# Rows h and -h added and subtracted ahead of the transform along h; that transform in 64x64 tiles, and one signal per unit in the second mixing

## What is computed

```python
residual = x
h = layer_norm(x, n1_g, n1_b)
xf = rfft2(h, axes=(1, 2), norm='ortho')          # 65 frequencies along w, 128 along h
# eight blocks of 16 channels, complex:
o1r = relu(xr @ w1[0] - xi @ w1[1] + b1[0]);  o1i = relu(xi @ w1[0] + xr @ w1[1] + b1[1])
o2r = softshrink(o1r @ w2[0] - o1i @ w2[1] + b2[0]);  o2i = softshrink(o1i @ w2[0] + o1r @ w2[1] + b2[1])
y = irfft2(o2r + 1j * o2i) + h
h = y + residual
residual = h
h = layer_norm(h, n2_g, n2_b)
return gelu(h @ mw1 + mb1) @ mw2 + mb2 + residual
```

## Time and profile before

| what | value |
|---|---|
| median of 3 runs | 1629.3 us (1629.04 to 1630.48) |
| the profiled execution | 1629.48 us |
| its span in the profile | 1627.7 us |
| TensorE matmul busy | 1556.1 us, 96% of the span |
| VectorE busy | 990.3 us, 61% |
| ScalarE busy | 889.3 us, 55% |
| POOL busy | 620.4 us, 38% |
| DMA, mean | 85 GB/s |

### The profile page before, as it was taken

How to read it: one execution, slowest core, us unless ns; L and a number is a source line. 1 busy time by engine, 2 the same in 40 slices (tenths; PEclk the granted TensorE clock), 3 DMA queues, 4 the chain that set the end, 5 groups by cost and what they waited for, 6 DMA issues and landing times.

```text
span 1627.7 us, 43919 instructions
## 1 busy us (share of the span) xinstructions
PE 1556.1 (96%) x16132; PEld 1379.1 (85%) x16132; DVE 990.3 (61%) x2433; ACT 889.3 (55%) x1638; POOL 620.4 (38%) x782
## 2 busy tenths in 40 slices
PE   0999999999999899999999989999999989999999
PEld 0987888888998788888898888888889879888888
DVE  7967556656537665665655766565663675555553
ACT  5544366666534356666643436666662443666665
POOL 5800046776800017677660003667673000111111
PEclk9999999999999999999999999999999999999999
DMA  8410713333300062333420052333331006011111
GB/s 225 172 45 3 241 49 107 104 99 119 98 15 3 9 240 86 108 101 99 124 79 2 3 203 66 104 110 97 104 111 46 3 3 207 27 39 32 32 39 46
DMA packets 168583, 138.30 MB, mean 85 GB/s; under 512 B 10882, under 2 KB 132484, under 8 KB 168452
## 3 DMA queue, kind: packets, MB, share of 16 engines
q1 hardware_dynamic: 167268, 136.24, 26.6%
q10 hardware_dynamic: 1184, 0.20, 0.1%
HBM read 69.30 MB, written 67.11 MB: 84 GB/s over the span
## 4 chain that ended last, share of the span: by engine, by line
PE 93%; DVE 3%; ACT 1%; SPq 1%; DMA 1%; issue 1%; POOL 0%; ACTq 0%; DVEq 0%
PE ps L797 27%; PE ps L591 8%; PE ps L611 8%; PE ps L581 7%; PE ps L763 7%; PE ps L765 7%; PE ps L724 7%; PE ps L764 7%; PE ps L757 3%; PE ps L649 3%; PE ps L743 3%; PE ps L749 3%; SPq L431 1%; DMA first<-in_x_dram 1%; PE ps L779 1%
## 5 line engine op out<-in xcount | busy, mean ns | idle before, releaser
L797 PEld LDWEIGHTS ps<-mw,gel 128*128 128x128 f32 x4000 | 520.6, 191 | 42.3
L797 PE MATMUL ps<-mw,gel 128*128 128x128 f32 x4000 | 523.7, 274 | 0.0
L907 ACT ACTIVATE gel<-ps,mb1f 128x512 f32<-128x512 f32 x500 | 343.7, 687 | 250.6 <-PE ps L765 219.7
L1473 POOL TENSOR_TENSOR arena<-arena,mb2rep 128x512 f32<-128x512 f32 x125 | 160.2, 1282 | 634.5 <-ACT hn L893 634.5
L763 PE MATMUL ps<-hth,mw1h 128*128 128x512 f32 x512 | 259.7, 507 | 4.5 <-DVE vsb L1119 1.7
L1462 POOL TENSOR_SCALAR arena<-xnext,rstd,shift 128x128 f32<-128x128 f32 x360 | 159.4, 462 | 207.6 <-DVE shift L1356 207.6
L893 ACT ACTIVATE hn<-arena,shift,rstd 128x128 f32 (+1 forms) x512 | 221.6, 483 | 16.8 <-DVE shift L1356 16.8
L765 PE MATMUL ps<-hth,mw1l 128*128 128x512 f32 x512 | 202.1, 395 | 0.0
L764 PE MATMUL ps<-htl,mw1h 128*128 128x512 f32 x512 | 200.8, 392 | 0.0
L1203 DVE TENSOR_TENSOR arena<-ps,arena 128x512 f32 (+1 forms) x60 | 41.5, 691 | 252.0 <-PE ps L749 233.4
L871 ACT COPY gsb<-ps 128x512 f32<-128x512 f32 x128 | 69.1, 589 | 159.1 <-PE ps L611 153.0
(11 more groups left out here) (111 smaller groups left out, 2125.6 us busy)
## 6 DMA issues: line engine op xcount, KB each, us to landing
arena<-aside SPq DMA_DIRECT2D x128, 256.0 KB, 4.8
aside<-gz SPq DMA_DIRECT2D x96, 256.0 KB, 3.0
between<-xout SPq DMA_DIRECT2D x62, 256.0 KB, 2.3
out_dram<-xout SPq DMA_DIRECT2D x62, 256.0 KB, 2.3
xnext<-between SPq DMA_DIRECT2D x60, 256.0 KB, 3.0
aside<-first SPq DMA_DIRECT2D x32, 256.0 KB, 2.3
xnext<-in_x_dram SPq DMA_DIRECT2D x30, 256.0 KB, 3.1
first<-in_x_dram SPq DMA_DIRECT2D x1, 960.0 KB, 7.4
```

The costliest lines, as they stand in the source:

```text
L797: mm = pe.matmul(ps[:, r % 2, P * i:P * i + P], gel[:, r % 2, m, P * i:P * i + P], mw2[:, s // IMAGES, m, :], start=(m == 0 and i == 0), s ...
L907: act.activation(gel[:, r % 2, m, :], ps[:, 2 + m % 2], ACT.Gelu, bias=mb1f[:, s // IMAGES, m:m + 1]).then_inc(gelu_out, 1)
L1473: pool.tensor_tensor(t, t, b, ALU.add).then_inc(mb2_done, 1)
```

## The change

- In steps 1 to 3 the slots 64 to 127 of an image are written in mirrored order (`zplace`, and the row order in `z_rows`, `scale` and VectorE's last tiles), so that slot 64 + i holds the row that is minus the row of slot i. The inverse constants are mirrored too, and the second half of the inverse transform along w reads its rows forward.
- The transform along w of steps 1 to 3 (`mirrored`) makes, for each four channels of both halves of the spectrum's rows, one bank from the slots 0 to 63 and one from the slots 64 to 127. Each matmul has 64 stationary columns, and two of them (g = 0 and 1) fill the two halves of the bank's partitions.
- ScalarE copies the first bank of the two to `hn` as it is (`upper_copy`), and VectorE writes the sum and the difference of that copy and the second bank into the spectrum (`fold_out`, two operations for each pair of banks). TensorE waits for VectorE's signal alone.
- The transform along h of steps 1 to 3 works on 64 partitions of sums and 64 of differences with the constants `FOLDS` (65 and 95 columns), in 64x64 tiles, for both units of a pair at once. It waits once, for both copies. The first two units are still done one by one.
- `mix2` uses banks 4 and 5 for q = 0 and 6 and 7 for q = 1, signals each unit, and waits for the first `shrink` operation of the same q in the pair before. `edges` stands ahead of mix2(4), whose second unit waits for VectorE's `edges_out`.
- The order of the frequencies along h is even ones first, then odd ones. The held products use banks 2 and 3, and `idft_h` waits for their GELUs.
- Step 0 keeps the transform along w and the 128x128 transform along h as they are.

The core of the diff:

```diff
@@ -73,8 +73,10 @@
 MASKS = 4 * BLOCKS
-CONSTS = 7 * P + MASKS
 EVEN = KWS + 1
+FOLD_E, FOLD_O = EVEN, P - EVEN + KWS // 2
+MASK_AT = 7 * P + FOLD_E + FOLD_O
+CONSTS = MASK_AT + MASKS
...
@@ -90,7 +92,7 @@
 HELD = TILES - 1
-HELD_BANK = (6, 7, 0, 2)
+HELD_BANK = (2, 3, 0, 2)
...
@@ -111,10 +113,18 @@
     fw[:, 0, 1] = cos[:, KWS]
-    fh = np.concatenate([np.cos(turn * np.outer(h, k)), np.sin(turn * np.outer(h, k[1:-1]))], 1) * scale
-    k_of = np.concatenate([k, -k[1:-1]])
+    ks = np.concatenate([[0, KWS], np.arange(2, KWS, 2), np.arange(1, KWS, 2)])
+    fh = np.concatenate([np.cos(turn * np.outer(h, ks)), np.sin(turn * np.outer(h, ks[2:]))], 1) * scale
+    k_of = np.concatenate([ks, -ks[2:]])
+
+    fold_e, fold_o = fh[:HALF, :EVEN].copy(), fh[:HALF, P - FOLD_O:].copy()
+    fold_e[-1] = scale * (ks % 2 == 0)
+    fold_o[:, :KWS // 2] = 0
+    fold_o[-1] = -scale * (np.arange(FOLD_O) < KWS // 2)
+    folds = np.tile(np.concatenate([fold_e, fold_o], 1), (2, 1))
     ih = np.concatenate([np.cos(turn * np.outer(k_of, h[:HALF + 1])),
                          np.sin(turn * np.outer(k_of, -h[HALF + 1:]))], 1) * scale
+    ih[:, HALF:] = ih[:, :HALF - 1:-1].copy()
 
...
@@ -182,6 +192,7 @@
         paired = [a.rearrange("p (t h e) -> p t h e", h=H, e=2) for a in flat]
...
@@ -207,7 +222,8 @@
         FW, FH, IH, DE, DO, IDENT, REVERSE = (cst[:, i * P:(i + 1) * P] for i in range(7))
-        mask = cst[:, 7 * P:].rearrange("p (s b) -> p s b", s=4)
+        FOLDS = tuple(cst[:, 7 * P + a:7 * P + b] for a, b in ((0, FOLD_E), (FOLD_E, FOLD_E + FOLD_O)))
+        mask = cst[:, MASK_AT:].rearrange("p (s b) -> p s b", s=4)
...
@@ -378,6 +394,11 @@
             return rows_of(s)[:, :, bass.ds(h0, ROWS), :].rearrange("p t h e -> p h t e")
+
+        def zplace(j, r):
+
+
+            return (2 * j + r // 2 + TILES // 2) * ROWS if r % 2 else tile_of(j, r) * ROWS
...
@@ -556,10 +577,8 @@
                     pe.wait_ge(a_act, cg + 1)
-                elif cg % 2:
-                    pe.wait_ge(a_dve, CGROUPS // 2 * (s - 1) + cg // 2 + 1)
-                else:
-                    pe.wait_ge(a_act, CGROUPS + CGROUPS // 2 * (s - 1) + cg // 2 + 1)
+                else:
+                    pe.wait_ge(a_dve, CGROUPS * (s - 1) + cg + 1)
...
@@ -573,8 +592,9 @@
                 for cg in range(CGROUPS):
-                    if s and cg == 3:
-                        pe.wait_ge(lo_out, TILES * s)
+                    if s:
+                        mirrored(s, cg // 2, cg % 2)
...
@@ -582,7 +602,45 @@
                                        start=True, stop=True)
                     mm.then_inc(s1_mm, 1)
 
-            def dft_h(s, n):
+            def mirrored(s, d, sign):
+
+                if d == 1 and sign:
+                    pe.wait_ge(lo_out, TILES * s)
+                if d >= 2 and not sign:
+                    evicted(s, 2 * d - 3)
+                q, slots = d // 8, slice(HALF, H) if sign else slice(0, HALF)
+                for i in range(GROUP):
+                    for g in range(2):
+                        t = KWS // 2 * q + KWS // 4 * g + GROUP // 2 * (d % 8) + i // 2
+                        mm = pe.matmul(ps[HALF * g:HALF * g + HALF, 2 + 2 * (d % 2) + sign, P * i:P * i + P],
+                                       rows_of(s)[:, t, slots, i % 2], FW, start=(i == 0), stop=True,
+                                       skip_group_check=True)
+                mm.then_inc(s1_mm, 1)
+
+            def dft_h(s, n, units=(0,)):
+                if s:
+                    g = spectrum_of(n + units[-1])
+                    if g >= 2:
+                        pe.wait_ge(g_out, 2 * BATCHES * s + g - 1)
+                    for i in range(GROUP):
+                        for o in range(2):
+                            for u in units:
+                                q = (n + u) % 2
+                                for x in range(2):
+                                    own_rows = slice(HALF * x, HALF * x + HALF)
+                                    cols = slice(HALF * (x ^ q), HALF * (x ^ q) + HALF)
+                                    dst = slice(P * i, P * i + EVEN) if o == 0 else slice(P * (i + 1) - FOLD_O, P * (i + 1))
+                                    mm = pe.matmul(ps[cols, q, dst],
+                                                   folded_of(s)[own_rows, GROUP * (g // 2) + i, o, q].rearrange(
+                                                       "p r c -> p (r c)"),
+                                                   FOLDS[o][own_rows], start=(i == 0 and o == 0), stop=True,
+                                                   skip_group_check=True)
...
@@ -635,20 +693,22 @@
                 kws = 1 if p == 1 else GROUP
-                if s == 0 and p == 1:
-                    pe.wait_ge(r_dve, R_DVE)
-                if p >= 2:
-                    pe.wait_ge(v_out, UNITS * s + 2 * p - 2)
                 for q in range(2):
+                    if p:
+                        pe.wait_ge(v_out, UNITS * s + 2 * p + q - 1)
+                    elif s == 0 and q:
+                        pe.wait_ge(r_dve, R_DVE)
+                    if p == EDGE_PAIR and q:
+                        pe.wait_ge(y_done, (UNITS + 1) * s + 2 * EDGE_PAIR + 1)
                     pe.wait_ge(o_out, UNITS * s + 2 * p + q + 1)
                     for i in range(kws):
-                        at_ = GROUP * HALF * q + HALF * i
+                        at_ = HALF * i
                         for c in range(2):
                             for g in range(2):
                                 own_rows, k = slice(HALF * g, HALF * (g + 1)), slice(HALF * c, HALF * (c + 1))
-                                mm = pe.matmul(ps[k, 4 + 2 * (p % 2) + g, at_:at_ + HALF], osb[own_rows, q, i, k],
+                                mm = pe.matmul(ps[k, 4 + 2 * q + g, at_:at_ + HALF], osb[own_rows, q, i, k],
                                                w2s[own_rows, q].rearrange("p r c -> p (r c)"), start=True, stop=True)
-                mm.then_inc(m2_mm, 2)
+                    mm.then_inc(m2_mm, 1)
 
...
@@ -660,25 +720,21 @@
                 mix1(s, 0)
-                for q in range(2):
-                    dft_h(s, 4 + q)
+                dft_h(s, 4, (0, 1))
                 for p in range(PAIRED):
                     if p + 1 < PAIRED:
                         mix1(s, p + 1)
-                    if p == EDGE_PAIR + 1:
-                        pe.wait_ge(y_done, (UNITS + 1) * s + 2 * EDGE_PAIR + 2)
-                    mix2(s, p)
                     if p == EDGE_PAIR:
                         edges(s)
+                    mix2(s, p)
                     if p + 3 < PAIRED:
-                        for q in range(2):
-                            dft_h(s, 2 * p + 6 + q)
+                        dft_h(s, 2 * p + 6, (0, 1))
                 if s:
                     fc1_held(s, 0)
                     fc1_held(s, 1)
                 else:
                     pe.wait_ge(v_out, UNITS * s + UNITS - 2)
-                    keep_warm(8, 6)
...
@@ -719,6 +775,8 @@
                         turned(s, cg - 4)
+                    elif s and cg >= 2:
+                        pe.wait_ge(gelu_out, CHUNKS * (TILES * s - 1) + cg - 1)
...
@@ -864,6 +922,11 @@
 
+            def upper_copy(s, q, j, r):
+
+                act.wait_ge(s1_mm, CGROUPS * s + CGROUPS // 2 * q + 4 * j + 2 * r + 1)
+                act.copy(hn[:, r].rearrange("p a b -> p (a b)"), ps[:, 2 + 2 * r]).then_inc(a_act, 1)
+
...
@@ -929,11 +992,17 @@
                     act.wait_ge(mb2_done, TILES * s)
-                for q in range(2):
-                    for g in range(2):
-                        with act.Fori(0, CGROUPS // 16) as j:
-                            for r in ((0, 2) if s else range(4)):
-                                a_out(s, q, g, j, r)
+                if s == 0:
+                    for q in range(2):
+                        for g in range(2):
+                            with act.Fori(0, CGROUPS // 16) as j:
+                                for r in range(4):
+                                    a_out(s, q, g, j, r)
+                else:
+                    for q in range(2):
+                        with act.Fori(0, CGROUPS // 8) as j:
+                            for r in range(2):
...
@@ -1087,9 +1156,15 @@
 
-            def a_out(s, q, g, j, r):
-                dve.wait_ge(s1_mm, CGROUPS * s + CGROUPS // 2 * q + CGROUPS // 4 * g + 4 * j + r + 1)
-                evict_a(dve.tensor_copy, s, q, g, 4 * j + r, r).then_inc(a_dve, 1)
+            def fold_out(s, q, j, r):
+
+                dve.wait_ge(a_act, CGROUPS + CGROUPS // 2 * (s - 1) + CGROUPS // 4 * q + 2 * j + r + 1)
+                dve.wait_ge(s1_mm, CGROUPS * s + CGROUPS // 2 * q + 4 * j + 2 * r + 2)
+                upper = hn[:, r].rearrange("p a b -> p (a b)").rearrange("p (i k r) -> p k r i", i=GROUP, r=2)
+                lower_ = ps[:, 3 + 2 * r].rearrange("p (i k r) -> p k r i", i=GROUP, r=2)
```

(43 more changed lines are left out.)

45 lines of the change are left out of this document (23 added, 22 removed).

## The result

The changed kernel takes 1639.8 us (median of 4 runs, 1636.66 to 1640.32) against 1629.2 us on the same chip. The ratio is 1.0059, 95% interval 1.0042 to 1.0077: about 10 us slower, where 1613.5 us and "faster" were forecast.

What follows compares the result with a forecast made beforehand. TensorE, busy 96% of the span, was taken as the bound, with ScalarE's chain next in the filter's pairs. 12.2 + 0.7 - 0.2 + 1.9 + 1.4 = 16.0 us off 1629.5 gave 1613.5 us; range 1602 to 1626.

Steps and rivals of the forecast that it cites:

- The step that failed: Transform along w, steps 1 to 3: VectorE's sum and difference fit under TensorE's time; the stage nets 1.4 us won.
- second rival: Transform along w: VectorE's sum and difference, 1.2 us each, become the bound; 33 us more, 1646 us; chance 0.05.
- the way to mix1(0): From the start of the transform along w to the first mixing, steps 1 to 3: 1.3 us lost in all.
- Mixing to `idft_h`: Filter from mix1(0) to the start of `idft_h`, steps 1 to 3: 17.4 us won in all.
- Undisturbed pairs: Filter's middle pairs, steps 1 to 3: from 4.79 to 4.41 us, bound by ScalarE's copies and relus; 12.2 us won.
- the prediction's own signs of being wrong: TensorE waiting for VectorE in most bank pairs, a pair at 4.0 or 4.8 us, or first mixing waiting for copies.
- First rival: Transform along w: 128-row column tiles run one after another, 90 us more in three steps, 1705 us; chance 0.05.
- Third rival: Folded transform along h: bound by issue, 1.6 us, pair stays 4.78 us, 12.2 us gone, 1625.5 us; chance 0.06.
- Fourth rival: Filter's pairs: ScalarE's chain does not bind, a pair falls to TensorE's 3.98 us, kernel 1599 us; chance 0.06.
- Edges: Edges in the filter: 0.1 us won in each of steps 1 to 3, 0.5 lost in step 0; net loss 0.2.
- Tail: End of the filter, all four steps: a signal for each unit starts the inverse 0.47 us earlier; 1.9 us won.
- Step 2: Transform along w in step 2: weight scaling between the halves stalls TensorE for some 0.6 us.

Runs made afterwards that it cites:

- Experiment 1: The changed kernel with ScalarE's copy writing `hn` in the order in which VectorE reads it: 1619.84 us, ratio 0.9942 to the kernel before.
- experiment 10: experiment 5 run once more, on the chip of experiment 9: 1609.43 us, ratio 0.9874.
- experiment 5: Experiment 1 without the 95-column half of the folded transform along h, from the third pair on in steps 1 to 3: 1609.58 us, ratio 0.9876.
- experiment 6: experiment 5 with ScalarE's relus working on half the columns in all steps: 1588.35 us in a single execution.
- experiment 3: The kernel before with only the second mixing's part (banks by q, signal per unit, edges ahead of mix2(4), held products in banks 2 and 3): 1630.59 us.
- experiment 8: Experiment 1 run once more, on the chip of experiment 7: 1619.48 us, ratio 0.9934.
- experiment 7: Experiment 1 with the edges back behind mix2(4), written to the unused upper half of bank 6: 1618.37 us, ratio 0.9933.
- experiment 9: experiment 5 with the left-out matmuls issued again, each with one column instead of 95: 1616.49 us, ratio 0.9927.

## Why the prediction was wrong

- **The step that failed: "128x512 with two operands takes 690 ns, also where it writes strided, so 1.5 us with addressing, under the 1.85 us that TensorE needs for two banks."** The row writes short runs and reads SBUF in plain order; the new operation also reads SBUF with neighbours 512 bytes apart, and no row had that. It took 1070 ns, a bank pair 2.14 us. This is the second rival, "VectorE's sum and difference become the bound", given 0.05 and 1.2 us an operation; its threshold of 0.93 us agrees with 1070 ns, where TensorE waited, and 684, where it did not. Its cost: the way to mix1(0) lost 17.4 us where 1.3 were forecast, so 16 us. Experiment 1 gets 6.4, 6.5 and 6.4 us back in this stretch of the steps 1 to 3, 19.3 of the 20.0 us between its median and the changed kernel's.
- **The other step that failed: the filter's instructions were costed at nothing beyond their matmuls.** The pairs were to be 4.41 us all through, with "stalls of up to 1 us a step" in the range, and no term for bringing 6144 instructions more. In their place are TensorE's stops: 14 waits for the next 256 instructions, 6.7 us in the waits view of the profiled execution. Mixing to `idft_h` was to win 5.8 us a step. It won 4.9, 3.2 and 1.9 in the changed kernel, and 6.4 to 6.8 in each step of experiment 10 (77.59 / 77.14 / 77.36 us), which has half of the folded transform and few stops. Together 7.4 us short.
- The two misses, 16.0 and 7.4, make 23.4 us; the profiled execution is 23.2 above the forecast.
- **Undisturbed pairs: right.** 4.39 us for 4.41, with ScalarE's cycle as a bound of it (experiments 5 and 6). The folded transform took 1.35 us, not 1.18, both for one unit (475.97 in the timeline, 32 records) and for two (511.47 in the chain, 64 records, 21 ns each). The forecast scaled the 64-column rate. The first mixing in the chain waits for copies and the transform rather than for relus, one of the prediction's own signs of being wrong: by the prediction's own sum 1.35 us would have made the pair 4.53 us (523.42 + 1.35 - 520.24). The transform started 3.04 us behind the first mixing (508.43 to 511.47), not the 3.18 of the prediction, so that the pair came out so near is in part luck.
- **First rival (128-row column tiles one after another): refuted.** 512 records in 28.15 us once VectorE keeps up; two side by side take 110 ns where one 128x128 record took 118. The forecast's 29.5 us was 1.35 too careful.
- **Third rival (issue at 25 ns a record): refuted** as priced, 21 ns a record. The number of instructions does cost, but in blocks of 256 and not for each record.
- **Fourth rival (3.98 us a pair):** reached only with the relu halved, 3.96.
- **Edges:** the loss in step 0 was 0.72 us (mix1 101.44 to 107.81, 6.37 us, for 5.65), not 0.5; experiment 3 shows the same 0.7 where the transform isn't shortened. **Tail:** 0.46 us a step (549.17 to 557.17 is 8.00, for 8.46), forecast 0.47. What followed the filter did not move, as costed.
- **Step 2:** forecast as a stall of 0.6 us; it lost 2.0 more than its neighbours (40.26 for 38.27), and 1.9 in experiment 1 (33.78 for 31.86), so VectorE's scaling of the weights costs this with either read order.

What stays open: why one stop is 0.3 and another 1.45 us was not worked out, and how much time the stops cost beyond the 6.7 us that the waits view shows. No kernel was made that has the same work in fewer instructions. That the stops grow from step 1 to step 3 in the changed kernel is one execution's order; in experiment 8 step 3 is no worse than step 1 (80.77 / 82.83 / 80.90 us from mix1(0) to `idft_h`).

## What to carry to other kernels

A duration from the trace holds for the access pattern of its row, each operand and the output apart: before costing a new operation by such a row, compare the innermost stride of all of them, and where VectorE reads SBUF in steps of 16 bytes or more, count 1.57 times for it (1073 for 684 ns). A permutation that someone must do was free on a read of PSUM and dear on VectorE's read and ScalarE's write of SBUF, so put it on the read of PSUM. And splitting matmuls into small tiles multiplies instructions: where TensorE issues one in 14 ns for long, as here, look for idle time whose releaser is "issue" and hold it against the packets of the instruction queue, since it can eat what the smaller tiles win.

## What was unexpected in the hardware

- VectorE's two-operand 128x512 f32 operation: 684 ns with neighbours 4 or 8 bytes apart in the SBUF operand that it reads, 1073 ns at 16, 1075 at 32 and 1070 at 512. ScalarE's copy writing SBUF: 585, 649 and 1092 ns for 4, 8 and 16 bytes apart. Both read PSUM in steps of 512 bytes at no cost.
- Two 128x64 tiles run side by side with 128 columns each at 55 ns a record, two in 110 ns.
- TensorE's stream of small float32 matmuls, 320 instructions in 4.39 us (13.7 ns each; before 224 in 4.79, 21 ns), stops for 0.2 to 1.45 us at a time, 4.5 to 7.2 us in a kernel (the waits view of the experiments 1, 7, 8 and 9). Each stop ends 1.24 to 1.60 us after a packet of 256 instructions has landed. The runs of these kernels differ by 3.4 to 5.5 us where the kernel before has 2.
